# A two-layer mixture-of-experts kernel: sorted rows kept as two 16-bit parts, normalisations in paired steps, experts chosen from logits

## The reference, cut to what matters

```python
# layer 0: attention pooling with one of three masks, then all 8 experts for every token
x = x + ffn0(pool(x, type_ids))        # gates = logits above the k-th value of all 16384, tanh gelu
# layer 1, first an adapter chosen by the sequence's language
h   = relu(x @ W1[lang] + b1[lang])
xa  = x + h @ W2[lang] + b2[lang]
x2  = layernorm(xa) * gamma[lang] + beta[lang]
# then a top-2 mixture of 8 experts
xn  = layernorm(x2) * gamma + beta
p   = softmax(xn @ gate_w);  w, idx = top_k(p, 2);  w = w / sum(w)
out = sum_k w_k * expert_idx_k(xn) + x2        # erf gelu
x   = x + out
```

## Time and profile before

| | |
|---|---|
| runs | 386.85 us median of 3 (386.45 to 387.94) |
| profiled execution | 388.65 us, of which the span from first to last instruction is 386.8 us |
| PE busy | 353.4 us (91%), mean granted clock 0.965 |
| DVE, ACT, POOL busy | 263.0, 256.2 and 226.6 us (68, 66 and 59%) |
| chain that ended last | PE 57%, DVE 13%, POOL 12%, issue 11% |

### The profile page before, as it was taken

The page is one execution under the profiler, slowest core; times in us unless marked ns, Lnnn a source line. Parts: engine busy times, 40 slices in busy tenths (PEclk is TensorE's granted clock), DMA queues, the critical chain, the costliest instruction groups (busy, mean ns, idle before and its releaser), DMA issues.

```text
span 386.8 us, 7491 instructions
## 1 busy us (share of the span) xinstructions
PE 353.4 (91%) x2092; PEld 203.7 (53%) x2093; DVE 263.0 (68%) x760; ACT 256.2 (66%) x451; POOL 226.6 (59%) x211
## 2 busy tenths in 40 slices
PE   8997999999999999969879786979999899999982
PEld 6765554444444454544445342437978787444430
DVE  0467748877649986757977757317798985367661
ACT  2465477877867657948794472649889898756650
POOL 6499999100026888717555786733378460287884
PEclk9999999999999999989998896969999999999998
DMA  7749922620066763642540111121324225631221
GB/s 204 256 104 371 399 89 67 179 43 0 9 169 140 144 128 72 151 93 70 100 120 17 58 43 35 47 71 44 109 76 128 67 69 90 157 94 42 66 57 54
DMA packets 47456, 40.94 MB, mean 106 GB/s; under 512 B 6978, under 2 KB 41522, under 8 KB 47290
## 3 DMA queue, kind: packets, MB, share of 16 engines
q1 hardware_dynamic: 44632, 36.12, 34.7%
q0 software_dynamic: 1760, 3.71, 3.3%
q10 hardware_dynamic: 1026, 0.65, 0.5%
HBM read 28.80 MB, written 11.67 MB: 105 GB/s over the span
## 4 chain that ended last, share of the span: by engine, by line
PE 57%; DVE 13%; POOL 12%; issue 11%; DMA 2%; ACT 2%; POOLq 0%; SPq 0%; DVEq 0%; ACTq 0%
PE bank L640 12%; POOL whl L1820 6%; PE bank L589 6%; PE bank L591 6%; PE bank L590 6%; PE bank L651 3%; PE bank L652 3%; PE bank L653 3%; POOL acc L767 3%; DVE l L699 2%; PE bank L566 2%; PE bank L1037 1%; PE bank L1341 1%; PE bank L1090 1%; PE bank L568 1%
## 5 line engine op out<-in xcount | busy, mean ns | idle before, releaser
L675 ACT ACTIVATE h<-bank,b1f 128x512 f32<-128x512 f32 x160 | 105.2, 686 | 84.1 <-PE bank L640 61.3
L699 DVE SCALAR_TENSOR_TENSOR l<-h 128x512 f16<-128x512 f32 x118 | 93.3, 794 | 20.7 <-ACT h L687 16.0
L767 POOL TENSOR_TENSOR acc<-acc,tmp 128x512 f32<-128x512 f32 x47 | 69.9, 1487 | 62.4 <-DVE tmp L740 60.0
L640 PE MATMUL bank<-h,w 128*128 128x512 f32 x160 | 83.3, 603 | 0.0
L687 ACT ACTIVATE h<-h 128x512 f16<-128x512 f32 x108 | 67.9, 629 | 2.1
L589 PE MATMUL bank<-xh,whl 128*128 128x512 f16 x128 | 49.3, 385 | 0.0
L591 PE MATMUL bank<-xh,whl 128*128 128x512 f16 x128 | 49.2, 385 | 0.0
L590 PE MATMUL bank<-xl,whl 128*128 128x512 f16 x128 | 49.2, 385 | 0.0
L1820 POOL DMA_INDIRECT whl<-sorted_out,idx x24 | 24.1, 1006 | 24.6 <-DMA sorted_out<-yo 18.3
L640 PEld LDWEIGHTS bank<-h,w 128*128 128x128 f32 x160 | 30.7, 195 | 11.6 <-issue 0.6
L669 ACT ACTIVATE h<-bank,b1f 128x256 f32<-128x256 f32 x76 | 31.4, 474 | 4.8 <-PE bank L568 2.6
(11 more groups left out here) (225 smaller groups left out, 710.1 us busy)
## 6 DMA issues: line engine op xcount, KB each, us to landing
Gs<-gates SPq DMA_DIRECT2D x40, 256.0 KB, 5.1
wraw<-in_w SPq DMA_DIRECT2D x16, 512.0 KB, 3.8
sorted_in<-zer SPq DMA_DIRECT2D x14, 448.0 KB, 6.7
wraw<-sorted_in SPq DMA_DIRECT2D x19, 128.0 KB, 2.2
sorted_out<-yo SPq DMA_DIRECT2D x19, 128.0 KB, 1.8
first<-in_xtm SPq DMA_DIRECT2D x1, 1024.0 KB, 8.9
mg<-in_gbc SPq DMA_DIRECT2D x8, 128.0 KB
w<-in_w SPq DMA_DIRECT2D x8, 128.0 KB, 2.8
```

The lines of the kernel that those rows point to most:

```text
L640: pe.matmul(o[:, :], w2[:, e, j * 128:j * 128 + 128], h32[:, u % NH, :], start=(c == 0), stop=(c == 3))\
L675: act.activation(h32[:, u % NH, :], bank[u % 4][:, :], ACT.Gelu if layer else ACT.Gelu_apprx_tanh, bias=b1f[layer][:, e * 4 + c:e * 4 + c ...
L699: dve.scalar_tensor_tensor(l16[:, slot(u), :], h32[:, u % NH, :], HS, h16[:, slot(u), :], ALU.mult, ALU.subtract).then_inc(s_lo, 1)
L767: pool.tensor_tensor(a, a, tmp[:, i % NTMP, :], ALU.add).then_inc(s_acc, 1)
```

## The change

Seven things are changed.

1. The order by hand: `PLACE` has new positions for every group. For group 2 the nT transpose goes from 10.3 to 10.9, the logits stay near 12.3, the rank matmul goes from 15.8 + 0.75 to 13.55 + 0.75, the h matmul from 1.7 to 1.6, and `act_h` from 2.0 to 1.5.
2. Each normalisation is two DVE steps of one kind of instruction: (x - mean) * gamma, which needs no reciprocal root, and then * root + beta. `scale` and `shift` are gone from POOL. The last gamma and beta, times XS = 16, are applied here too, from a broadcast copy `fgr` that is 128 x 256.
3. The rows to be sorted are split before the scatter: ACT writes the high 16-bit part, POOL the low part, into `xs`; a row stays 512 bytes. A tile is then turned by four 16-bit transposes into one PSUM bank and comes out with one DVE copy; lines 1775, 1782 and 1786 are gone.
4. Experts are chosen from the logits: no softmax, no exponential on ACT. POOL computes e to the power d.
5. `pe_rank` waits for the one-hot sums and counts (`m_oh`), not for the weights, which come later (`weights()`).
6. The last addition to `acc` of each group's layer 0 is DVE's and follows its `gated` instruction.
7. POOL waits, ahead of `pool_loads`, for the identity matrix and rounds it to 16 bits; the w2 loads have a semaphore for each expert.

```diff
-PLACE = [
-    {"lg": 17.6, "d": 17.2, "exp": 17.4, "top": 17.8, "rank": 24.5, "scatter": 9.7},
-    {"h": 2.0, "act_h": 2.2, "lg": 17.6, "d": 17.2, "exp": 17.4, "top": 17.8, "rank": 22.5, "scatter": 2.9},
-    {"h": 1.7, "act_h": 2.0, "xa": 3.0, "stats": 3.1, "rstd": 3.6, "n1": 4.6, "stats2": 6.2, "rstd2": 6.0, "n2": 8.3,
-     "x2T": 11.3, "x2a": 11.8, "nT": 10.3, "xn": 10.5, "lg": 12.2, "d": 11.8, "exp": 12.3, "top": 13.4, "rank": 15.8,
-     "scatter": 2.0},
-    {},
+MID = {
+    "h": 1.6, "act_h": 1.5, "xa": 3.1, "stats": 3.6, "rstd": 4.4, "s1": 4.6, "s2": 5.6, "stats2": 6.7, "rstd2": 7.6,
+    "n2a": 7.8, "n2": 8.9, "nT": 10.9, "xn": 10.4, "hi": 10.5, "lo": 11.0, "lg": 12.3, "d": 11.5, "top": 11.7,
+    "rank": 13.55, "e": 13.5, "w": 16.6, "x2T": 12.9, "x2a": 13.2, "cT": 20.5, "scatter": 2.0,
+}
+LATE = {
+    "h": 1.5, "act_h": 1.5, "xa": 3.3, ..., "nT": 13.5, ..., "lg": 15.3, "d": 14.5, "top": 14.7,
+    "rank": 17.2, "e": 16.4, "w": 20.6, "x2T": 16.9, "x2a": 17.2, "cT": 24.5, "scatter": 2.0,
+}
+PLACE = [LATE, MID, MID, {"s1": 5.5, "s2": 7.5, "n2a": 10.2, "lg": 17.6, "d": 17.2, "top": 17.8, "e": 19.0, "w": 21.5}]
...
-            at("pool", pos + AT["add"], add(i, kind, v))
+            if i + 1 in done0.values():
+                at("dve", pos + 0.05, add(i, kind, v))
+            else:
+                at("pool", pos + AT["add"], add(i, kind, v))
...
-            def dve_n1(dve):
+            def dve_s1(dve):
...
+                    last = dve.scalar_tensor_tensor(n1[...], o[...], mv[:, 0, i, 0:1],
+                                                    gbc[:, 2 * g + i // 2, 0:D], ALU.subtract, ALU.mult)
+            def dve_s2(dve):
...
+                    last = dve.scalar_tensor_tensor(x2[...], n1[...], rs[:, 0, i:i + 1],
+                                                    gbc[:, 2 * g + i // 2, D:2 * D], ALU.mult, ALU.add)
...
+            def act_rows(act):
+                act.wait_ge(m_n2, g + 1)
+                act.activation(rows_of(0), n2f[...], ACT.Copy).then_inc(m_xh, 1)
+
+            def pool_rows(pool):
+                pool.wait_ge(m_xh, g + 1)
+                pool.tensor_tensor(rows_of(1), n2f[...], rows_of(0), ALU.subtract).then_inc(m_xs, 1)
...
-            def act_exp(act):
-                act.wait_ge(m_d, g + 1)
-                act.activation(ex[:, :, :], lg[:, :, :], ACT.Exp).then_inc(m_e, 1)
+            def pool_e(pool):
+                pool.wait_ge(m_dd, g + 1)
...
+                pool.tensor_tensor(ee[:, :], base[:, :], dd[:, :], ALU.pow).then_inc(m_e, 1)
...
-                pe.wait_ge(m_cw, g + 1)
+                pe.wait_ge(m_oh, g + 1)
...
             def pe_t(pe):
-                for z in range(2):
-                    last = pe.transpose(o[:, z * 128:z * 128 + 128], xr[:, i % NX, z, :], ident[:, :])
+                for k in range(2):
+                    for z in range(2):
+                        c = k * TS + z * 128
+                        last = pe.transpose(o[:, c:c + 128], xr[:, i % NX, z, k * D:k * D + D], ident16[:, :])
...
-            def act_x(act):
...
-            def dve_x(dve):
...
-            def pool_x(pool):
...
+            def evac_x(eng):
                 if i >= NX:
+                    eng.wait_ge(s_m1, US + 2 * (i - NX) + 2)
+                eng.wait_ge(t_tr, i + 1)
+                o = bank[mb[("t", i)][0]][:, :].bitcast(F16)
+                eng.tensor_copy(xt[:, i % NX, :], o[:, 0:2 * TS]).then_inc(t_xl, 1)
...
+            pool.memset(base[:, :], float(np.float32(np.e)))
             link(pool, "pool", pool.memset(mhalf[:, :], -0.5))
+            pool.wait_ge(ld["ident"], 16)
+            pool.tensor_copy(ident16[:, :], ident[:, :]).then_inc(t_zm, 1)
```

More of the change, by code:

```diff
@@ L314, in build_adaln_ffn @@
         s_w16 = sem("s_w16")
-        s_w2b = sem("s_w2b")
+        s_w2b = [sem(f"s_w2b{e}") for e in range(E)]
         s_w2f = sem("s_w2f")
@@ L384, in build_adaln_ffn @@
         m_e = sem("m_e")
+        m_dd = sem("m_dd")
         m_cw = sem("m_cw")
@@ L1370, in rstd @@
                 return fn
-            def dve_n1(dve):
+            def dve_s1(dve):
                 o = bank[mb[("xa", g)][0]]
+                dve.wait_ge(m_mv, g + 1)
+                if g == 0:
+                    dve.wait_ge(ld["lang"], 16 * 4 * B)
+                else:
+                    dve.wait_ge(m_n2, g)
+                for i in range(4):
+                    last = dve.scalar_tensor_tensor(n1[:, i * 128:i * 128 + 128], o[:, i * 128:i * 128 + 128], mv[:, 0, i, 0:1],
+                                                    gbc[:, 2 * g + i // 2, 0:D], ALU.subtract, ALU.mult)
+                last.then_inc(m_n1, 1)
@@ L1527, in _, with weights, part @@
                         def _(dve, i=i):
-                            return dve.tensor_tensor(cumb[:, i + 1, :], cumb[:, i, :], OB[:, i, :], ALU.add)
+                            ins = dve.tensor_tensor(cumb[:, i + 1, :], cumb[:, i, :], OB[:, i, :], ALU.add)
+                            if i == 4 * g + 3:
+                                ins.then_inc(m_oh, 1)
+                            return ins
+                return parts
+            def weights():
+                parts = []
+                def part(fn):
+                    parts.append(fn)
                 @part
                 def _(dve):
+                    dve.wait_ge(m_oh, g + 1)
+                    dve.wait_ge(m_e, g + 1)
+                    return dve.tensor_scalar(c4[:, :, 0], ee[:, :], 1.0, None, ALU.add)
+                @part
+                def _(dve):
+                    return dve.reciprocal(wk[:, :, 0], c4[:, :, 0])
+                @part
+                def _(dve):
+                    return dve.tensor_tensor(wk[:, :, 1], ee[:, :], wk[:, :, 0], ALU.mult)
+                @part
+                def _(dve):
+                    if g:
+                        dve.wait_ge(m_cT, g)
+                    if g < GA:
+                        dve.tensor_copy(wA[:, sl, :], wk[:, :, :])
                     for k in range(2):
@@ L1567, in mid @@
             at("pool", m + after("rstd", g), rstd(0, m_mv, m_rs))
-            at("dve", m + after("n1", g), dve_n1)
-            if g == GA - 1:
-                spread("dve", "dve", m + after("n1", g) + AT["x2d"], 0.15, [scale, shift])
-            else:
-                spread("pool", "pool", m + AT["x2"], 0.01, [scale, shift])
+            at("dve", m + after("s1", g), dve_s1)
+            at("dve", m + after("s2", g), dve_s2)
             spread("dve", "dve", m + after("stats2", g), 0.15, stats(x2, 1, m_mv2, ready2))
             at("pool", m + after("rstd2", g), rstd(1, m_mv2, m_rs2))
+            at("dve", m + after("n2a", g), dve_n2a)
             at("dve", m + after("n2", g), dve_n2)
+            if g < GA:
+                at("act", m + after("hi", g), act_rows)
+                at("pool", m + after("lo", g), pool_rows)
             at("pe", mpos[("x2T", g)], pe_x2T)
@@ L1581, in mid @@
             at("pe", mpos[("lg", g)], pe_lg)
-            at("dve", m + after("d", g), dve_d)
-            at("act", m + after("exp", g), act_exp)
-            spread("dve", "dve", m + after("top", g), 0.15, top())
+            at("dve", m + after("d", g), dve_lg)
+            spread("dve", "dve", m + after("top", g), 0.15, choice())
+            at("pool", m + after("e", g), pool_e)
+            spread("dve", "dve", m + after("w", g), 0.15, weights())
             at("pe", mpos[("cT", g)], pe_cT)
```

184 lines of the change are left out of this document (80 added, 104 removed), and 2 rows, old and new, of the table LATE.

## The result

The changed kernel took 382.59 us (median of 4 runs, 380.07 to 382.84) against 386.65 us on the same chip: ratio 0.9876, interval 0.9827 to 0.9925. It is faster, by 4.1 us. The ratios leave out the few executions that were over 1.5% slower than the fastest of the same kernel; the medians count them. The prediction said 374.0: right in sign, a third of the size, and at the place of rival B. A second series on another chip gave 382.2 us, 0.9855 [0.9805, 0.9905].

What follows compares the result with a forecast made beforehand. PE was taken as the bound, busy 91% of the span, with some 28 us of waits and low clock between 160 and 272 us. -13.0 + 0.8 - 0.5 = -12.7 us gave 374 us; own range 369 to 379, 8 in 10 364 to 383.

Steps and rivals of the forecast that it cites:

- rival B: DVE late nearly everywhere by a little: longer waits at nT and rank, more clock falls; 382 us, chance 0.15.
- steps 2 to 6: Between 160 and 272 us: 15.2 of 28.2 us of waits and lost clock stay, so 13.0 us are gained.
- additions, small waits: DVE's last additions wait for POOL's, plus remaining short waits for DVE: 1.5 us left, bounds 0 and 3.
- step 2: Paired normalisation, groups 1 and 2: chain from statistics to nT 9.1 to 11.2 us, 2.0 us of waits left.
- Step 1: No exponential: without table loads on ACT, PE's two waits for hTs go, 5.2 us; 0 to 1.5 us may stay.
- Rival C: Paired steps of groups 1 and 2 meet POOL's scatters, 2.1 us more a step; slower, 390 us, chance 0.07.
- Step 3: Choice from logits and earlier rank, groups 0 to 2: PE waits 1.2 us ahead of each rank, 3.6 us.
- Step 4: Tile start: rank to first transpose stays 16.4 us, first transpose to first product 2.5 us; 3.1 us of waits left.
- Step 6: PE's clock, 160 to 272 us: 5.0 of 11.7 us of loss stays, bounds 2 and 9.
- Step 7: Prologue: POOL's loads behind the identity matrix delay PE's first unit; 0.8 us lost, bounds 0 and 2.
- Step 8: Tile stretch: 0.5 us off PE's waiting; ACT busy 39 us, DVE 47.6 to 52.9 of 55 us.

Runs made afterwards that it cites:

- experiment 1: Kernel before, its four exponentials written as copies so that no table is loaded: 381.3 us, 0.9809.
- 12: One unused exponential of 4 numbers put back per group: into the changed kernel 384.1 us, 0.9858; into 7's kernel 385.3 us, 0.9939.
- experiment 3: Changed kernel without the 16 scatters of groups 0 and 1: 374.1 us, 0.9606.
- 7: Changed kernel, scatters moved in POOL's queue, six of group 0's behind POOL's addition preceding DVE's own last: 378.05 us, 0.9777; again 378.7 us, 0.9746.
- 10: 7's kernel, group 1's scatters spread further, group 0's transposes, logits, choice and rank 1.5 units later, its weights later too: 374.9 us, 0.9661.
- 11: 10's kernel with no scatter ahead of group 1's first root and one instead of two ahead of group 2's: 376.4 us, 0.9711.
- Experiment 13: First normalisation of groups 0 and 1 made as before, unpaired: in the changed kernel 384.6 us, 0.9863; in 11's kernel 380.5 us, 0.9800.
- experiment 4: Kernel before without its 16 scatters of groups 0 and 1: 381.5 us, 0.9836.
- Experiment 14: Changed kernel with the copy of each tile out of PSUM made twice: 386.2 us, 0.9917.
- 6: Changed kernel with 14 of the 16 scatters of groups 0 and 1 at other places in POOL's queue: 381.2 us, 0.9824.
- 8: Changed kernel with the scatters of groups 0 and 1 at their places from before the change: 381.7 us, 0.9847.
- 9: 7's kernel with group 0's transposes, logits, choice and rank 1.5 units later, its weights behind group 1's chain: 381.8 us, 0.9890.

## Why the prediction missed

The prediction left 15.2 us of 28.2 in steps 2 to 6. The same places in the profile after:

```
                                       left, predicted   left, measured
2  waits for n2f                             2.0              7.8
3  waits ahead of rank                       3.6              2.8
4  start of the tiles                        3.1              4.8
5  additions, small waits                    1.5              0.4
6  clock, 160 to 272 us                      5.0              8.3
sum                                         15.2             24.1
```

Row 2 counts group 0's wait of 1.95 us, which step 2 didn't look at and which lies just ahead of 160 us. Clock after: 0.07 x 70 + 0.08 x 26 + 0.08 x 16 = 8.3 us. The difference is 8.9 us; tiles and tail gained 2.9 more than forecast, and the start lost 0.7 more. 8.9 - 2.9 + 0.7 = 6.7 us, and the predicted span (386.8 - 12.7 = 374.1) was missed by 6.6. The other 2 us between 374.0 and the median are those that I took off for the profiled execution of before, which lay 1.8 above its median; the one of after lay at its own.

- **Step 1** had the outcome right, all waits for hTs went, and its mechanism half. Without the loads, in the old order, 2.6 of the 5.2 us stayed (experiment 1). With the loads put back in the new order no wait for hTs came back (12): the new order takes them away by itself, and which of its places does was not tried. The price of 5.2 us was low for the loads by themselves (7 us in experiment 1, 6.6 in 12), since the clock falls behind such waits and PE waited elsewhere too; in the changed kernel the gain mostly hides behind the other waits: put back there, the exponential moved the median by 1.5 to 1.9 us, between chips, and the ratio not measurably.
- **Step 2 is the step that failed.** It took the chain from a group's statistics to its nT transpose as 9.1 to 11.2 us, because "POOL's two roots now run beside it". Measured were 13.5 us in group 1 and 13.7 in group 2, where it was 13.6 before. The step overlooked the in-order queue, though it said itself that scatters lie "on POOL, ahead of its roots", and priced that at 1.0 us a group. The waits were 3.35 and 2.52 us, and 1.95 us in group 0. Without the scatters of groups 0 and 1 the two chains took 12.5 and 11.6 us (experiment 3). Of these 3.1 us the paired steps' own durations make 0.5; the rest is time between instructions, such as the 4.3 us that group 2's root stood behind its input. Order alone took 3.5 us off the kernel (7), and with room for group 0 also, 7.3 us (10). With no scatter ahead of group 1's first root and one ahead of group 2's the chains took 12.7 and 11.2 us (11), so the upper bound was reached in one group. Not all was the queue: without those scatters 4.6 us of waits for n2f stayed, 1.92 of them in group 0. Experiment 13 (4 us for the first pair of groups 0 and 1) says that this pair is worth having; the second pair was not undone.
- **Rival B** stands at the measured time by luck. It wanted 4.0 us of waits at nT in groups 1 and 2 and 6.6 ahead of rank, and there were 5.9 and 2.8; it had 8.0 us for the clock (8.3), and the 2.9 us that the tiles gave were not in it.
- **Rival C**, the steps meeting the scatters, was right in size for one step of six (2.87 us) and half for another (1.87 us), and wrong in what they meet. In all 20 traces a step that reads two SBUF tensors is long only beside an addition of POOL. The row behind rival C (2.96 us) had an addition of 1.27 us beside it as well as a scatter, and took 2.06 us when the scatters of groups 0 and 1 were left out (experiment 4). The Trainium skill (GPSIMD Engine Reference, "Key points") names DVE instructions in a two-port mode or with two SBUF inputs as those that contend with POOL. The trace agrees for the additions: the step that reads PSUM (L1389) took 1.12 us in group 0 beside an addition, and the next one there, with two SBUF inputs, took 3.16 beside POOL's three:

```profile
145.99 1.12 DVE L1389 SCALAR_TENSOR_TENSOR n<-bank,mv,mg 128x128 f32<-128x128 f32 x4
146.01 4.49 POOL L773 TENSOR_TENSOR acc<-acc,tmp 128x512 f32<-128x512 f32 x3
147.75 3.16 DVE L1400 SCALAR_TENSOR_TENSOR x<-n,rs,mg 128x128 f32<-128x128 f32 x4
```

- **Step 3** was right, 1.41 us a wait for 1.2, twice instead of three times in this execution (three times in the second series).
- **Step 4** was 1.7 us short, in both of its parts. From the first transpose to the first product it took 252.88 - 249.28 = 3.6 us, not 2.5 (3.5 before): PE waited 0.7 and 0.9 us for the rows of tiles 1 and 2 and 0.7 us for the copy, so the shorter path through DVE gained nothing there (timeline of PE):

```profile
249.28 0.38 PE L1811 MATMUL bank<-ident,wraw 128*128 128x128 f16 x4 [2.51 <-DMA wraw<-sorted_in]
250.37 0.38 PE L1811 MATMUL bank<-ident,wraw 128*128 128x128 f16 x4 [0.71 <-DMA wraw<-sorted_in]
251.68 0.50 PE L1811 MATMUL bank<-ident,wraw 128*128 128x128 f16 x4 [0.92 <-DMA wraw<-sorted_in]
252.88 0.39 PE L572 MATMUL bank<-xt,first 128*128 128x256 f16 x1 [0.70 <-DVE xt L1819]
```

Rank to first transpose took 249.28 - 231.12 = 18.2 us, not 16.4. Indices came later, because on DVE stood a gated term, a low part and a product that took 1.15 us beside POOL's addition (0.29 in group 1); the scatters began 3.2 us behind the rank (1.7 before).
- **Step 6** was 3.3 us short because of step 2: the clock fell behind each of the three waits for n2f.
- **Step 7**: the first dense unit came 0.6 us later, 0.8 predicted. **Step 8** was too low by 2.9 us. In its stretch ACT was busy for 43.8 us, not 39, and DVE for 44.5, below the 47.6 to 52.9. The step said that DVE's instructions would shorten without POOL's low parts and priced that at nothing; they did: a low part took 705 ns instead of 738, and three small instructions of group 3's placing 0.16 to 0.18 us instead of 0.66 to 0.70. The copy took the lower of its bounds,

```profile
L1819 DVE COPY xt<-bank 128x512 f16<-128x512 f16 x19 | 7.9, 417 | 3.7 <-PE bank L1811 3.7
```

417 ns against 415 for 256 elements of 32 bits. The perf-mode rule of the Trainium skill (VectorE: DVE Perf Modes, "The perf-mode tier table"), up to twice the rate out of PSUM for 16 bits, agrees with this. Experiment 14's trace shows that DVE's time in the tiles does count: 7.9 us more cost 5.1 us there. That the gain comes from DVE's load rather than from ACT and POOL, which also lost work, was not tried by itself.

Left open: how the 3.4 us of tiles and tail divide between engines. PE's idle time from the first tile's transpose to its last instruction fell by 2.3 of them, from 7.1 to 4.8 us; the waits for DVE's low parts (1.6 us) are gone and the one for `mo` went from 1.8 to 0.9. The start of the span differs by up to 3.5 us between executions of equal prologues (135.3 to 138.8 us). Both executions at 138.8 us, of experiments 1 and 7, had a fall of the clock near 34 us, of 6.8 and 3.4 us at 0.50, which is worth 3.4 and 1.7 us; one of experiment 4, with 3.4 us of it, started at 136.4. The rest stays open.

## What to carry to other kernels

When a step is freed from an input that another engine makes, look at what that engine has in its queue when the input falls due: here the roots stood behind scatters, and 7.3 of the 9 missing us came back by moving positions alone. A gain measured in one kernel isn't a gain in another where a different wait ends last: the exponential was worth 7 us, nothing that the ratios resolve (1.5 us by the medians), and 6.6 us in three orders of the same work. After each reordering read the waits again before judging the idea: experiments 6, 8 and 9 removed the wait that they aimed at and each made a new one of over 5 us.

## What the runs showed of the hardware

- TensorE's granted clock behind a wait. Over all 20 profiled executions, between 130 and 242 us, of 46 waits of PE from 1.3 to 1.9 us none was followed within 4 us by a lower clock, of 26 from 1.92 to 2.8 us 14 were, and of 17 of 2.88 us and more 16 were (in the longest it fell before they ended); it was then at 0.50 (1.2 of 2.4 GHz) for some 3.4 us, and for up to 7 us behind the longest. The exception was a wait of 3.67 us. As an estimate from these, a wait of 3 us costs nearer to 5: 3.4 us at half the clock lose 1.7.
- A step of four instructions of 128 x 128 on DVE that reads two SBUF tensors is lengthened by POOL's additions and not by its scatters alone. Over all 20 profiled executions, up to 260 us: 68 such steps had no addition beside them and took 1.12 to 1.14 us, 25 of them beside a scatter for 0.3 us or more; the 64 with 0.3 us or more of an addition beside them took 1.70 to 3.16 us, and the 10 of these that had a scatter beside them too 2.57 to 2.88. The 47 steps that read PSUM took 1.11 or 1.12 us, whatever lay beside them (an addition for 16, a scatter for 25).
- A scatter grows beside DVE's long instructions with two SBUF inputs: in the changed kernel to 2.43, 1.90 and 1.85 us, each time beside one of 128 x 1024 elements (L905, 1.2 us).
- A scatter of 128 rows of 512 bytes takes POOL 0.96 us and 0.30 us of idle time behind it, so eight in a row hold the queue for 10 us.
